# A retention block and a mixture of experts on one core: the seam between the two phases written in a new order

## The reference

```python
x = x + attn(layernorm(x))          # phase one
x = x + moe(layernorm(x))           # phase two
# attn: 16 heads of 16 channels; r, k, v, g are projections of a mix of each token with the one before
#   per chunk: y = (r k * Wmat) v + (r state) * wb ;  state = ws * state + (k * wk) v
#   y normed per head, scaled, times gelu(g), projected by Wo
# moe: 8 experts, top 2 of softmax(x @ gate.T), at most 320 tokens of a sequence in each expert
#   h1 = d @ w1 ; h3 = d @ w3 ; out = (silu(h1) * h3) @ w2   (256 -> 896 -> 256)
#   final[token] += prob * out
```

## Time and profile before

| what | value |
| --- | --- |
| median of 3 runs | 855.15 us (853.99 to 855.53) |
| the profiled execution's own time | 854.25 us |
| its span (first to last instruction record) | 852.2 us |
| PE busy | 812.1 us, 95% |
| DVE, ACT, POOL busy | 499.1, 490.7, 462.0 us |
| granted PE clock over the span | 0.993 of full speed |

### The profile page before, as it was taken

One profiled execution on the slowest core, in us unless ns is written; L12 is line 12 of the kernel. 1 busy time (PEld: TensorE's weight loads), 2 busy tenths in 40 slices (PEclk: granted clock), 3 DMA queues, 4 the chain that ended last, 5 costly groups with the idle time before them and its releaser, 6 DMA issues. The chain is left out here.

```text
span 852.2 us, 17481 instructions
## 1 busy us (share of the span) xinstructions
PE 812.1 (95%) x6343; PEld 677.2 (79%) x6343; DVE 499.1 (59%) x1237; ACT 490.7 (58%) x876; POOL 462.0 (54%) x497
## 2 busy tenths in 40 slices
PE   3999999999999998999999999999999999999995
PEld 2678887777788776787997788997788898888884
DVE  6888888899888767343542443543543544443441
ACT  4578888888888787354643543643543543552431
POOL 6454476777787756475434355434356443436214
PEclk9999999999999999999999999999999999999998
DMA  5852132113111122654334145333334342404113
GB/s 149 342 196 70 34 117 74 52 52 96 42 50 65 53 78 75 208 157 82 101 67 91 59 106 94 100 68 40 109 95 72 92 110 28 121 2 51 20 14 42
DMA packets 50474, 74.05 MB, mean 87 GB/s; under 512 B 5056, under 2 KB 42176, under 8 KB 50368
## 3 DMA queue, kind: packets, MB, share of 16 engines
q1 hardware_dynamic: 35488, 53.46, 19.1%
q0 software_dynamic: 14592, 19.18, 13.5%
q10 hardware_dynamic: 288, 0.01, 0.0%
HBM read 38.41 MB, written 34.22 MB: 85 GB/s over the span
## 5 line engine op out<-in xcount | busy, mean ns | idle before, releaser
L1592 POOL DMA_INDIRECT out<-ysb,index x80 | 124.7, 1559 | 145.3 <-DVE ysb L1831 111.5
L1945 PE MATMUL p<-xh,whi 128*128 128x512 f32 (+2 forms) x504 | 185.6, 368 | 6.1 <-issue 5.2
L1807 DVE TENSOR_TENSOR hid<-gated,p 128x512 f32<-128x512 f32 (+1 forms) x126 | 81.1, 643 | 181.1 <-ACT gated L1654 181.1
L1947 PE MATMUL p<-xh,wlo 128*128 128x512 f32 (+2 forms) x504 | 185.3, 368 | 0.0
L1946 PE MATMUL p<-xl,whi 128*128 128x512 f32 (+2 forms) x504 | 184.6, 366 | 0.0
L1971 PE MATMUL py<-w,hh 128*128 128x512 f32 x448 | 162.6, 403 | 3.7 <-DVE hl L1088 3.0
L1654 ACT ACTIVATE gated<-p 128x512 f32<-128x512 f32 (+1 forms) x126 | 71.0, 564 | 162.2 <-PE p L1947 162.2
L1581 POOL TENSOR_TENSOR wlo<-wraw,whi 128x448 fp32r<-128x448 f32 x56 | 70.7, 1266 | 94.7 <-ACT whi L1640 90.6
L1945 PEld LDWEIGHTS p<-xh,whi 128*128 128x128 f32 x504 | 94.7, 188 | 23.4 <-issue 8.0
L1970 PE MATMUL py<-w,hl 128*128 128x256 f32 x384 | 108.6, 283 | 0.0
L1946 PEld LDWEIGHTS p<-xl,whi 128*128 128x128 f32 x504 | 94.8, 188 | 15.3
(11 more groups left out here) (204 smaller groups left out, 1440.4 us busy)
## 6 DMA issues: line engine op xcount, KB each, us to landing
wraw<-in_w SPq DMA_DIRECT2D x24, 896.0 KB, 4.8
disp<-wraw SPq DMA_DIRECT2D x16, 662.5 KB, 9.3
xtok<-disp SPq DMA_DIRECT2D x16, 530.0 KB, 4.9
x_ring<-in_x SPq DMA_DIRECT2D x16, 256.0 KB, 3.5
out<-x SPq DMA_DIRECT2D x16, 256.0 KB, 2.2
xtok<-disp SPq DMA_DIRECT2D x8, 265.0 KB, 4.2
out<-ysb,index POOLq DMA_INDIRECT x80, 3.8
disp<-row,slot_i POOLq DMA_INDIRECT x64
```

Source lines behind the costliest of these rows:

```text
L1592: nc.gpsimd.indirect_dma_start(out, bass.IndirectOffsetOnAxis(ap=index[e.const % 2][:, t:t + 1], axis=0), ysb[j % NY][:], None, compute_op ...
L1807: nc.vector.tensor_tensor(hid[k][:, 0:w], gated[k][:, 0:w], p3[k][:, 0:w], ALU.mult).then_inc(hid_ready, 1)
L1945: nc.tensor.matmul(dst[:, 0:w], hi[m][:, wcut], xh[xcut], start=(kt == 0), stop=False)
L1947: ins = nc.tensor.matmul(dst[:, 0:w], lo[m][:, wcut], xh[xcut], start=False, stop=(kt == KT - 1))
```

## The change: what it does

Four things are edited.

1. The hand-written end of phase one has another order on POOL, ACT, DVE and PE. Block 15's `group_rstd`, `scaled`, `normed_y`, `residual`, `stats2`, `norm2`, `normed2`, `turn2` and `logits` stand earlier, among block 14's steps. `state_b(15)`, whose result nobody reads, goes to the end. `early_up` can be issued by halves (`p1` first, then `p3`), and the first half waits for `gated_ready` alone.
2. The first two early output tiles are computed slice by slice (`early_downs`): slices 0 to 5 of tile 0, slices 0 to 5 of tile 1, then slice 6 of each. Each slice waits for its own low part instead of for all seven.
3. Three early tiles stand before the two turns, where there were two. The fourth early tile stands before `up` of chunk 2, where it stood behind it in both arms of the branch. ACT, DVE and POOL follow (`scale_out`, `sum_out`, `add`).

```diff
-            with nc.Block() as block:
+            with nc.Block(no_gpsimd_drain=True) as block:
...
         scatter(12)                                    # on_gpsimd
         chain.reset()
-        weight_low(9)
         norm2(14)
         gated(15)
+        weight_low(9)
+        norm2(15)
         scatter(13)
         chain.reset()
         early_index()
-        norm2(15)
         weight_low(11)
         scatter(14)
...
+        square_y(15)                                   # on_scalar
         keep_y(15)
-        square_y(15)
         turned2(13)
         early_hi(0)
         early_hi(1)
         group_log(15)
+        group_rstd(15)
         logit_exp(13)
+        scaled(15)
         early_gate(0)
-        group_rstd(15)
         normed2(14)
-        scaled(15)
         early_gate(1)
         early_hidden_hi(0)
         turned2(14)
-        early_gate(2)
         weight_high(11)
         early_hidden_hi(1)
+        normed2(15)
         logit_exp(14)
+        turned2(15)
+        early_gate(2)
         early_gate(3)
-        normed2(15)
+        logit_exp(15)
         early_hidden_hi(2)
-        turned2(15)
         early_hidden_hi(3)
-        logit_exp(15)
...
         stats2(14)                                     # on_vector
+        logit_max(13)
+        normed_y(15)
         best_two(13)
         tally(13)
         early_hidden(0)
-        normed_y(15)
+        residual(15)
+        stats2(15)
         slots(13)
...
         early_turn(1)                                  # on_tensor
+        group_sums(15)
         logits(13)
-        group_sums(15)
         early_up(0)
         early_up(1)
+        project_o(15)
         count(13)
-        early_up(2)
         turn2(14)
-        project_o(15)
+        early_up(2, (0,))
         logits(14)
-        early_up(3)
+        early_up(2, (1,))
+        early_up(3, (0,))
+        turn2(15)
+        early_up(3, (1,))
+        logits(15)
+        count(14)
         early_up(4)
-        count(14)
-        turn2(15)
-        logits(15)
-        early_up(5)
+        early_up(5, (0,))
         count(15)
+        early_up(5, (1,))
         early_up(6)
...
+        def early_downs(e, first_tile):
+
+            pe.wait_ge(wlo_ready, 3 * WP)
+            pe.wait_ge(x1_ready, STEPS)
+            w2 = split[0].w2
+            for part in (range(FT - 1), range(FT - 1, FT)):
+                for t in range(first_tile, first_tile + 2):
+                    to, off = py[tile_at(e, t)], (t - EARLY_T.start) * P
+                    for f in part:
+                        if t == first_tile:
+                            pe.wait_ge(hl_ready, f + 1)
+                        a, b = hh[0][:, f, off:off + P], hl[0][:, f, off:off + P]
+                        if f:
+                            nc.tensor.matmul(to[:, 0:C], b, w2[:, f, 0, :], start=False, stop=False)
+                        ins = nc.tensor.matmul(to[:], a, w2[:, f].rearrange("p h c -> p (h c)"), start=(f == 0), stop=(f == FT - 1))
+                        if not f:
+                            nc.tensor.matmul(to[:, 0:C], b, w2[:, f, 0, :], start=False, stop=False)
+                    if part[-1] == FT - 1:
+                        ins.then_inc(ffn_done, 1)
...
-            for t in range(t0, t0 + n - 2):            # on_tensor of phase two, first(e)
-                down(e, t)
+            early_downs(e, t0)
+            down(e, t0 + n - 2)
             for i in range(2, TB - 1):
                 turn(e, i)
-            down(e, t0 + n - 2)
+            down(e, t0 + n - 1)
             pe.wait_ge(taken_ready, 1)
             up(e, 2)
-            with_rest_where_taken(e, lambda: down(e, t0 + n - 1))
+            with_rest_where_taken(e, lambda: None)
             last_chunk(e)
```

More of the change, by code:

```diff
@@ L1138, in on_vector @@
         early_lo(0)
-        logit_max(13)
         early_lo(1)
         stats2(14)
+        logit_max(13)
+        normed_y(15)
         best_two(13)
@@ L1144, in on_vector @@
         early_hidden(0)
-        normed_y(15)
+        residual(15)
+        stats2(15)
         slots(13)
         chain.reset()
+        early_hidden(1)
+        logit_max(14)
         early_hidden_lo(0)
-        early_hidden(1)
         early_weight()
-        residual(15)
-        logit_max(14)
-        early_hidden(2)
-        stats2(15)
+        early_hidden_lo(1)
         best_two(14)
         tally(14)
-        early_hidden_lo(1)
+        logit_max(15)
+        early_hidden(2)
         slots(14)
@@ L1160, in on_vector @@
         early_hidden(3)
-        state_b(15)
-        logit_max(15)
-        early_hidden_lo(2)
         best_two(15)
         tally(15)
+        early_hidden_lo(2)
         early_hidden(4)
@@ L1171, in on_vector @@
         early_hidden_lo(4)
+        early_hidden_lo(5)
         early_hidden(6)
-        early_hidden_lo(5)
         early_hidden_lo(6)
+        state_b(15)
         nc.vector.tensor_tensor(taken[:], base[:], base0[:], ALU.subtract).then_inc(taken_ready, 1)
@@ L1354, in early_turn, with early_up @@
             ins.then_inc(turned, 1)
-        def early_up(f):
+        def early_up(f, parts=(0, 1)):
             if f == 0:
@@ L1362, in early_up @@
                 pe.wait_ge(ysq_ready, STEPS)
-            wait(pe, hid_ready, f - 1)
-            for m, dst in ((0, early_p1[f % 2]), (1, early_p3[f % 2])):
+            for m in parts:
+                dst = (early_p1, early_p3)[m][f % 2]
+                wait(pe, (gated_ready, hid_ready)[m], f - 1)
                 for kt in range(KT):
@@ L1369, in early_up @@
                     ins = nc.tensor.matmul(dst, split.up[1][m][:, wcut], kept.xh[:, kt, early_cols], start=False, stop=(kt == KT - 1))
-            ins.then_inc(h_done, 1)
+            if parts[-1] == 1:
+                ins.then_inc(h_done, 1)
         for c in range(-1, TAIL):
@@ L1463, in phase_b @@
     added = [sem(f"added{k}") for k in range(NY)]
-    taken_ready, x1_out = sem("taken_ready"), [sem(f"x1_out{k}") for k in range(2)]
+    taken_ready, x1_ready, x1_out = sem("taken_ready"), sem("x1_ready"), [sem(f"x1_out{k}") for k in range(2)]
     HPE = NCH * FT
@@ L1599, in first @@
                 pool.wait_ge(x1_out[k], 16 * STEPS // 2)
-            early = tile_order(e)[:CHUNKS[EARLY][1] - 1]
+            early = tile_order(e)[:CHUNKS[EARLY][1]]
             for t in early:
@@ L1742, in first @@
             t0, n = CHUNKS[EARLY]
-            for t in range(t0, t0 + n - 2):
+            for t in range(t0, t0 + n - 1):
                 scale_out(e, t)
@@ L1746, in first @@
                 turn_hi(e, i)
-            scale_out(e, t0 + n - 2)
+            scale_out(e, t0 + n - 1)
             act.wait_ge(taken_ready, 1)
             hidden(e, 2, [(m, q) for m in range(3) for q in range(WP)], 2)
-            owed = lambda: scale_out(e, t0 + n - 1)
-            with_rest_where_taken(e, owed, owed, REST)
+            with_rest_where_taken(e, lambda: None, lambda: None, REST)
             last_chunk(e, True)
@@ L1884, in first @@
                 turn_lo(e, i)
-            sum_out(e, t0 + n - 2)
+            sum_out(e, t0 + n - 1)
             for k in range(1, 3):
@@ L1893, in first @@
             hidden(e, 2)
-            owed = lambda: sum_out(e, t0 + n - 1)
-            with_rest_where_taken(e, owed, owed, REST)
+            with_rest_where_taken(e, lambda: None, lambda: None, REST)
             last_chunk(e, True)
```

## The result

The changed kernel takes **850.32 us** (median of 6 runs, 847.81 to 851.85) against 854.57 for the kernel before (6 runs on the same chip). The ratio is 0.9945, 95% interval [0.9928, 0.9961]. It is 4.2 us faster where 3.2 were forecast.

A forecast was written before the change was run, and what follows sets the result against it. PE was taken to set the end nearly everywhere, leaving its idle times, low clock and what follows its last matmul. Terms of -2.0, +1.8 and -3.0 gave -3.2 us from 855.15, so 851.9 us, range 848.8 to 854.6.

The forecast's parts named there:

- seam: Between phase one and the experts: turn 2.0 us earlier, 1.8 us lost again to the clock behind `up` of chunk 2.
- Term 1: At the join of the phases: the turn and `up` of chunk 2 start earlier, -2.0 us.
- PE chain: PE's matmuls less its waits, up to the turn: third early tile ends at 345.8, before the rows arrive.
- rows chain: Block 14 and 15 scatters, then SP's load: 2.0 us earlier, sets the turn at 346.6.
- Term 2: Behind `up` of chunk 2: moving the fourth early tile leaves 3.2 us idle and the clock falls, +1.8 us.
- Rival A: Behind `up` of chunk 2: the clock stays up despite the idle time, giving 850.1 us; chance 0.20.
- No stretch at half clock before it: Expected sign at the turn: it starts at 346 to 347 with no half-clock stretch ahead.
- Term 3: Behind POOL's last DMA: removing POOL's drain from the block's end saves time, -3.0 us, bounds 0 and 4.8.
- a branch with what stands behind it: At the kernel's end: 1.77 us at worst out of 4.8, leaving 3.0 for the drain.

The follow-up runs named there:

- old tail order: The changed kernel with phase one's last steps in the order of before, early tiles and new end kept: 851.53 us, ratio 0.9954.
- the changed kernel again: The changed kernel, unaltered, run once more on another chip: 850.84 us, ratio 0.9946 to the kernel before.
- the pair kernel: The changed kernel with the first two output tiles of expert 0's last chunk also done slice by slice: 846.63 us, ratio 0.9898; repeated on another chip, 0.9895.
- the drain by hand: The changed kernel with one hand-written drain of POOL behind its last DMA, block end still new: 855.70 us, ratio 1.0002 to the kernel before.
- the filled one: The changed kernel with unused transposes in two gaps, 12 before the first turn and 14 behind `up` of chunk 2: ratio 0.9950 to the kernel before.
- order only: The changed kernel with the old block end, drain included, put back: ratio 1.0012 to the kernel before.
- pair and fill: The pair kernel with 12 unused transposes of PE in front of the first turn: ratio 0.9898 to the kernel before.

## Why the prediction was right, and where it was not

The forecast was 851.9 us and the time 850.32, within the range. The sum of the forecast was a seam of nearly nothing (-2.0 + 1.8) and an end of -3.0. The runs show a seam of 0 to +1 us (ratios 1.0012 and 1.0002 with the old end) and an end of -4.4 to -4.9. That the total came within 1.6 us of the forecast is in part luck: the seam was too good in the forecast and the end too small, and the two errors cancel in part.

**Term 1, predicted -2.0, measured -1.1.** The mechanism was right: the rows set the turn, PE waits 0.94 in front of the third tile (0.8 predicted), the fourth tile is paid for in full. The PE chain was ready at 345.4 (345.8 predicted). The size was off in three links of the rows chain. `scatter(15)` started at 336.33 instead of 335.8. Its four DMAs took 5.4 us instead of 5.3. From SP's issue to the turn it took 4.05 us instead of 3.77. I had said that the last part "doesn't change"; the trace shows that it did, and not why.

**Term 2, predicted +1.8, measured +1.2.** The tile of chunk 2 starts 23.23 us behind `up` (23.26 predicted), behind hl. The gap was 3.0 us from the `turn` to the tile, of which 2.39 idle (3.2 predicted; another 0.53 us of idle time stands in front of that turn). The fall came, but earlier, in the idle time itself, and so less of it lay on matmuls: 3.86 us for the tile, not 4.3. This is one execution. In the traces with the old end and with the old tail order the fall came only on the tile's matmuls, which took 4.10 us, and in the changed kernel again it took 4.65, so the predicted price lies within what the traces show. Rival A had said that the fall doesn't follow from the gap's length alone. That much is borne out, by the waits of the last section, but its time is not: the clock fell here in every trace with the idle time unfilled. With 14 transposes in it, which leave 1.10 us idle, it stayed up in the one trace.

**"No stretch at half clock before it" was wrong in general.** The profiled execution has none. In three other executions of the same order (the changed kernel again, the pair kernel and the drain by hand) the turn and the tile behind it take 4.9 to 5.0 us instead of 3.4. The changed kernel again, PE in order of time and that stretch:

```profile
347.70 1.97 PE L1930 MATMUL pt<-ident,xtok 128*128 128x128 f32 x8 [1.90 <-DMA xtok<-disp]
352.67 0.39 PE L1948 MATMUL p<-xh,whi 128*128 128x512 f32 x1
```

```profile
347.70:352.67 4.97, 4.97 (x22) 4.57 (x23) 1.38 (x2) 1.17 (x2) 1.52 (x1) 0.66 1.07 329
```

So the change doesn't move one fall from the seam to behind `up`. It splits one idle time of 3.0 us into 0.9 and 2.0, behind which the clock may still fall, and adds another of 2.4, behind which it fell in every trace of that form but the filled one. In the traces, that is why the change without its end is no gain although the turn is earlier.

**Term 3, predicted -3.0, measured -4.8.** This is the term that was mis-sized. I gave 1.8 us of the empty 5.4 to "a branch with what stands behind it", from the earlier trace rows. In the changed kernel completion, branch and barrier together fit into the 0.8 us behind the last packets. The price of a branch of PE in the middle of its stream was the wrong row for a branch of POOL that has nothing behind it. The drain is nearly the whole stretch: 4.4 to 4.8 us by the traces, near my upper bound of 4.8. The Trainium skill (VectorE: DVE Perf Modes, "The DRAIN you can't avoid") puts the drains of a program's preamble and postamble at about 12 ns on all engines. It says this of drains that the runtime puts in. This one is the block's own, on POOL behind indirect DMAs, and its price is the measured one: 4.4 us (traces) to 4.9 us (medians) by the drain written by hand. The estimate of 1.6 us for the drain is not borne out either, which the prediction worked out from the fixed 2.0 us of the Trainium skill (DMA: Bandwidth & Descriptors, "Anatomy of one DMA — SWDGE (gpsimd) path"). Only 0.8 us lie behind the last packets, with completion and barrier in them. Whether a part of the 2.0 lies in or ahead of the packets' own time, no run separates.

**The fourth stretch, not predicted.** The 1.3 us between 387 and 842 us come for the most part from the waits of PE shown above, 4.7 us instead of 5.8. The changed kernel again had 5.4 for the same code and 455.81 for the stretch, so 0.9 of the 1.3 can be one execution against another. The rest is within what the fourth stretch varies in the table, and I put it to no edit. The table's four values above 456.5 (order only, old tail order, pair, pair and fill) are those of the traces in which the clock falls once in the expert loop.

## What to carry to other kernels

Look at the end first: when the last packets are over and the span still runs for microseconds, a drain of GpSimd may be all of it, and no tuning of the main loop reaches it. An idle time in which an engine waits for a transfer isn't shortened by making that engine faster: find the chain that sets the transfer, and put covering work where its absence is felt, behind the long block whose last product is late. There the same slice-wise loop that gave no measurable time at the seam was worth 4.2 us.

## What the hardware did that I had not expected

A drain of GpSimd behind indirect DMAs whose packets were over took 4.4 to 4.9 us, whether the block's own or one by hand. No run has such a drain without indirect DMAs before it, so what in it takes the time stays open. PE's issue waits behind the three branches of the loop last 1.5 to 1.9 us and vary between executions of the same code (4.7 and 5.2 us together). Behind one of 1.93 us in the pair kernel with fill the clock fell too, in the middle of the expert loop:

```profile
592.46 0.47 PE L1952 MATMUL p<-xh,whi 128*128 128x512 f32 x1 [1.93 <-issue]
```

```profile
592.46:598.00 5.54, 5.54 (x17) 4.41 (x18) 0.63 (x1) 0.60 (x1) 2.80 (x2) 0.69 0.44 52
```

Behind one of 1.77 us it had stayed up. So it did behind 1.88 us in the changed kernel again (1.00 from 724.88 on), while it fell behind 1.82 us in the pair kernel and in the kernel with the old end, and behind 1.86 us with the old tail order (0.69 over the next 5.5 us in each). So the length of the wait alone doesn't say whether the clock falls. These falls come with and without a fill at the seam, so filling one gap doesn't remove all of them.
